# A column layer's tile loop: rows turned two tiles ahead, output product two tiles behind

## What is computed

```
cols     = gelu(einsum('bsd,cdn->bscn', x, W_cols) + b_cols)     # 16 columns of 64 neurons
cols     = cols * weights[..., None]                             # one column kept per token
y        = cols.reshape(B, S, -1) @ proj_w + proj_b + x
out      = (y - mean(y)) * rsqrt(var(y) + 1e-05) * ln_g + ln_b
```

## Time and profile before

| | us |
|---|---|
| median of 3 runs (lowest, highest) | 1276.15 (1275.35, 1277.19) |
| the profiled execution's own time | 1278.38 |
| its span, first to last instruction | 1276.6 |
| the tile loop on PE, first transposes to the end of the last output product | 1165.8 to 1260.5 |
| last DVE instruction | ends 1268.2 |
| last store issued by POOL | 1269.4 |

### The profile page before, as it was taken

One profiled execution on the slowest core, in us unless ns is written; L12 is line 12 of the kernel. 1 busy time (PEld: TensorE's weight loads), 2 busy tenths in 40 slices (PEclk: granted clock), 3 DMA queues, 4 the chain that ended last, 5 costly groups with the idle time before them and its releaser, 6 DMA issues. The chain is left out here.

```text
span 1276.6 us, 33231 instructions
## 1 busy us (share of the span) xinstructions
PE 1180.1 (92%) x12565; PEld 852.2 (67%) x12565; DVE 963.9 (76%) x1677; ACT 674.7 (53%) x1497; POOL 587.9 (46%) x835
## 2 busy tenths in 40 slices
PE   4798899999999999589999999999999996998994
PEld 4575688778778778356666666666676664754662
DVE  7778656765765775878888888888888885776776
ACT  5854122123113113267788778877877775332673
POOL 1426888888888000543333333333333320815674
PEclk9998899999999999779999999999999999889997
DMA  8605444545545110785656566656666620434661
GB/s 219 160 1 187 123 145 137 173 137 145 168 136 164 47 37 1 113 146 95 96 92 96 98 99 99 99 99 99 99 98 99 97 40 2 116 116 143 196 183 43
DMA packets 111754, 141.82 MB, mean 111 GB/s; under 512 B 10317, under 2 KB 94776, under 8 KB 109380
## 3 DMA queue, kind: packets, MB, share of 16 engines
q1 hardware_dynamic: 97796, 96.15, 37.2%
q0 software_dynamic: 13824, 43.84, 12.0%
HBM read 105.79 MB, written 30.49 MB: 107 GB/s over the span
## 5 line engine op out<-in xcount | busy, mean ns | idle before, releaser
L1269 DVE TENSOR_REDUCE s_neg_max<-banks 112x3 bf16<-112x1461 f32 (+1 forms) x192 | 290.2, 1512 | 44.8 <-PE banks L1385 44.7
L1183 ACT ACTIVATE s_prob<-banks 128x448 f32<-128x448 f32 x512 | 272.8, 545 | 91.1 <-PE banks L1411 76.3
L714 DVE TENSOR_TENSOR s_m<-banks,s_base 128x512 f32<-128x512 f32 x256 | 161.2, 683 | 100.6 <-PE banks L868 100.3
L1411 PE MATMUL banks<-s_q_t,s_k_t 112*128 112x112 bf16 x2048 | 186.5, 215 | 1.1 <-ACT s_prob L1183 1.0
L1411 PEld LDWEIGHTS banks<-s_q_t,s_k_t 112*128 112x128 bf16 x2048 | 124.1, 98 | 72.6 <-issue 50.6
L868 PE MATMUL banks<-s_gate_sel,s_tw 64*128 64x256 f32 x1024 | 132.5, 399 | 1.3 <-DVE s_m L714 1.3
L911 PE MATMUL banks<-s_m,s_act_t 128*112 128x256 f32 x512 | 128.2, 388 | 1.5
L1427 PE MATMUL banks<-s_prob,s_v 128*32 128x112 f32 (+1 forms) x4096 | 125.8, 263 | 0.7 <-ACT s_prob L1183 0.7
L893 PEld LDWEIGHTS banks<-s_x_t,s_m 128*128 128x128 f32 x1024 | 116.7, 192 | 10.6 <-issue 7.6
L893 PE MATMUL banks<-s_x_t,s_m 128*128 128x112 f32 x1024 | 122.4, 278 | 0.0
L808 ACT ACT_TABLE_LOAD x8 | 10.3, 1283 | 206.5 <-PE banks L893 206.5
(11 more groups left out here) (312 smaller groups left out, 2209.7 us busy)
## 6 DMA issues: line engine op xcount, KB each, us to landing
k_parts<-s_k_split POOLq DMA_DIRECT2D x64, 281.2 KB, 3.6
s_k_t<-k_parts SPq DMA_DIRECT2D x32, 562.5 KB, 8.0
s_tw<-in_tw SPq DMA_DIRECT2D x16, 1024.0 KB, 5.3
s_k_raw<-in_ctx_k POOLq DMA_DIRECT2D x64, 187.5 KB, 3.7
s_k_t<-k_parts SPq DMA_DIRECT2D x32, 375.0 KB, 5.3
s_v_raw<-in_ctx SPq DMA_DIRECT2D x32, 256.0 KB
s_src<-in_ctx SPq DMA_DIRECT2D x8, 896.0 KB, 15.6
s_k_t<-k_parts SPq DMA_DIRECT2D x32, 187.5 KB, 9.0
```

The source lines that it names most:

```text
L714: nc.vector.tensor_tensor(dst[:, :, :, rows_], got, base[:, :, rows_].unsqueeze(2).broadcast_to([P, 2, B, HR]), ALU.add).then_inc(S["merge ...
L1183: nc.scalar.activation(prob[t % 2][:, c, :], w.bank(SCORE + n % SRING, P, TILE), ACT.Exp, scale=DH ** -0.5).then_inc(S["exp_done"], 1)
L1269: nc.vector.tensor_reduce(neg_max[half][:, ROWS + first:ROWS + end, 0], w.banks[0:T, MAX:MAX + end - first, 0:NKEY], AX.X, ALU.max, negate ...
L1411: last = nc.tensor.matmul(w.bank(SCORE + n % SRING)[:, s * T:(s + 1) * T], k_t[k][0:ROWS_MAX, h, c * P:(c + 1) * P], q_t[k][0:ROWS_MAX, h, :],
```

## The change

Evacuated rows (`x_tt`) and gelu outputs (`hid_c`) get three buffers each, the weights six. Transposes go to bank 0, 1 or 7, two tiles ahead of the column product; the output product comes two tiles behind it. The dummy matmuls move from the end of a turn into `turn`, ahead of the transposes, and write the bank that the transposes then overwrite. `column` and its waits, `SQRT_LAG`, the order on DVE and POOL and the dummy matmuls outside the loop stay.

```diff
-    SEMS, RING_W, N_SUBS = 8, 4, 2 * SLOT_TILES
+    SEMS, RING_W, DEEP, N_SUBS = 8, 6, 3, 2 * SLOT_TILES
...
-        x_tt = [sb(f"s4_x_tt{k}", [P, KD, P]) for k in range(2)]
+        x_tt = [sb(f"s4_x_tt{k}", [P, KD, P]) for k in range(DEEP)]
-        hid_c = [sb(f"s4_hid_c{k}", [N4, 2, P]) for k in range(2)]
+        hid_c = [sb(f"s4_hid_c{k}", [N4, 2, P]) for k in range(DEEP)]
...
+        def turned_at(n):
+
+            return w.bank((0, 1, 7)[n % 3])
+
+        def column_at(n):
+
+            return w.bank(2 + n % 2, N4, P)
...
-                for k in range(2):
+                for k in range(DEEP):
                     nc.gpsimd.memset(hid_c[k][:], 0.0)
...
                 def evacuate_row(n):
                     wait(act, "turned", n + 1)
-                    wait(act, "col_ps", n - 1)
+                    wait(act, "col_ps", n - DEEP + 1)
                     for kk in range(KD):
-                        last = nc.scalar.activation(x_tt[n % 2][:, kk, :], w.bank(n % 2)[:, kk * P:(kk + 1) * P],
+                        last = nc.scalar.activation(x_tt[n % DEEP][:, kk, :], turned_at(n)[:, kk * P:(kk + 1) * P],
...
                     wait(act, "col_ps", n + 1)
-                    wait(act, "y_ps", n - 1)
+                    wait(act, "y_ps", n - DEEP + 1)
...
                 evacuate_row(0)
+                evacuate_row(1)
                 for n in range(N_TILES):
-                    if n + 1 < N_TILES:
-                        evacuate_row(n + 1)
+                    if n + 2 < N_TILES:
+                        evacuate_row(n + 2)
                     gelu(n)
                     if n >= SQRT_LAG and group_end(n - SQRT_LAG):
                         roots(n - SQRT_LAG)
...
                 def turn(n):
                     pe.wait_ge(row_in[n % SEMS], 16 * (n // SEMS + 1))
-                    wait(pe, "x_tt_done", n - 1)
+                    wait(pe, "x_tt_done", n - 2)
+                    busy(2, turned_at(n))
                     for kk in range(KD):
-                        last = nc.tensor.transpose(w.bank(n % 2)[:, kk * P:(kk + 1) * P], row(n)[:, kk * P:(kk + 1) * P],
+                        last = nc.tensor.transpose(turned_at(n)[:, kk * P:(kk + 1) * P], row(n)[:, kk * P:(kk + 1) * P],
...
                 turn(0)
+                turn(1)
                 for n in range(N_TILES):
-                    if n + 1 < N_TILES:
-                        turn(n + 1)
+                    if n + 2 < N_TILES:
+                        turn(n + 2)
                     column(n)
-                    if n >= 1:
-                        output(n - 1)
-                    busy(2)
+                    if n >= 2:
+                        output(n - 2)
+                output(N_TILES - 2)
                 output(N_TILES - 1)
```

More of the change, by code:

```diff
@@ L1734, in gelu @@
                     wait(act, "col_ps", n + 1)
-                    wait(act, "y_ps", n - 1)
+                    wait(act, "y_ps", n - DEEP + 1)
                     for k, c in enumerate(cs):
                         at = slice(k * SUB, (k + 1) * SUB)
-                        last = nc.scalar.activation(hid_c[n % 2][:, k, at], w.bank(2 + n % 2, N4)[:, at], ACT.Gelu,
+                        last = nc.scalar.activation(hid_c[n % DEEP][:, k, at], column_at(n)[:, at], ACT.Gelu,
                                                     bias=b_cols[:, bass.ds(c, 1)])
@@ L1992, in _, with busy @@
                     last.then_inc(S["logit_ps"], 1)
-                def busy(count, cols=512):
+                def busy(count, bank=w.bank(7)):
                     for _ in range(count):
-                        nc.tensor.matmul(w.bank(7, P, cols), ones16[:], keep[:].rearrange("t c b -> t (c b)")[:, 0:cols],
-                                         start=True, stop=True)
+                        nc.tensor.matmul(bank, ones16[:], keep[:].rearrange("t c b -> t (c b)"), start=True, stop=True)
                 wait(pe, "counting", 2)
@@ L2043, in column @@
                         for kk in range(KD):
-                            last = nc.tensor.matmul(w.bank(2 + n % 2, N4)[:, at], w_tile[n % RING_W][:, k, kk, :],
-                                                    x_tt[n % 2][:, kk, at], start=(kk == 0), stop=(kk == KD - 1))
+                            last = nc.tensor.matmul(column_at(n)[:, at], w_tile[n % RING_W][:, k, kk, :],
+                                                    x_tt[n % DEEP][:, kk, at], start=(kk == 0), stop=(kk == KD - 1))
                     last.then_inc(S["col_ps"], 1)
@@ L2054, in output @@
                     for k, c in enumerate(cs):
-                        last = nc.tensor.matmul(w.bank(4 + n % 3, P, D), hid_c[n % 2][:, k, :], proj[:, bass.ds(c * D, D)],
+                        last = nc.tensor.matmul(w.bank(4 + n % 3, P, D), hid_c[n % DEEP][:, k, :], proj[:, bass.ds(c * D, D)],
                                                 start=(k == 0), stop=(k == 1))
```

## The result

The changed kernel takes 1280.82 us (median of 7 runs, 1278.53 to 1284.41), the kernel before beside it 1276.48. The ratio is 1.0039, 95% interval 1.0023 to 1.0055: slower by 5.0 us (2.9 to 7.0). Forecast: +2.9 us, 1279.0, range 1273.4 to 1282.3.

A forecast was written before the change was run, and what follows sets the result against it. PE was taken to bound the tile loop, after following the weights before column 8, with DVE the bound at the end. The terms summed to -1.6 + 6b, +2.9 us with b = .75: 1279.0 us, range 1273.4 to 1282.3.

The forecast's parts named there:

- One group with its roots: Tile loop: ACT waits at the root for DVE's later radicands, holding register loads; gelu 18 ends late, output 18 stalls .75 us.
- b: PE's stall ahead of an output, once per four-tile group, six between columns 8 and 33: .75 us, against .53 before.
- The value from the rows of an ordinary group: Choice of .75 us for the stall per group, between bounds of .2 and 1.3.
- Rival (3): Held chains in the loop are longer through slow register loads: stall 1.0 to 1.3 us, +4.4 to +6.2; chance .19.
- The start: Before column 8 weights come when they came, PE runs 1.2 us behind them, and column 8 stays at 1188.0.
- The end: After column 33 DVE decides: tile 33 is summed 6.0 us after it, 4.4 before; the longer lag gives back 1.6.
- past the last column: The stall of the group after those ending at 7 to 27 would fall after column 33, so it wasn't counted.
- DVE's chain is the same: From the summing of tile 33 on, DVE takes the same 12.0 us as before, the stores behind it.
- No cost of dummies and buffers: Loop: moved dummies taken as 0 (up to .54 us a turn if they collided); third buffers and their clearing cost nothing.
- Rival (1): ACT's register loads run during the root's wait: stall .2 us, sum -.4, 1275.7, no slower; chance .20.
- Rival (2): Start: weights come early enough that PE doesn't trail by 1.2 us; the stall vanishes too: -2.8, 1273.4; chance .11.
- The sum: Whole kernel: -1.6 + 6b us, with b = .75 +2.9 us; 1281.3 for the profiled execution, 1279.0 for the median.

The follow-up runs named there:

- e8: Changed kernel with roots three turns after a group's end up to tile 27 and outputs caught up to one behind from column 32: .9972, 1272.9 us.
- e6: Changed kernel with PE's two register loads for the output issued ahead of the column product's waits: .9981 of the kernel before, 1274.1 us.
- e11: Changed kernel with four weight buffers instead of six: 1.0062 of the kernel before.
- e10: Changed kernel with ACT's two register loads for the next gelu ahead of the root's wait, run again for its profile; first measured at 1.0011, 1277.9 us.
- e12: Changed kernel with PE's register loads ahead of the column's waits and outputs caught up to one behind from column 32: .9997, 1276.1 us.
- e7: Changed kernel with roots three turns after up to tile 27, PE's loads ahead of the column's waits, outputs caught up from column 32: .9993, 1275.6 us.
- e3: Changed kernel with output products one tile behind again, rows still turned two ahead: 1.0008 of the kernel before.
- e1: Changed kernel with roots taken three turns after a group's end instead of two: .9990 of the kernel before, 1275.2 us.
- e5: Kernel before with output products two tiles behind and three gelu output buffers, nothing else: 1.0529, 1344.27 to 1346.73 us.
- e9: Kernel before with outputs two behind, three gelu output buffers and more dummies in the first four turns: 1.0065, 1282.78 to 1288.12 us.

## Why the prediction was right, and where its sizes were off

- **One group with its roots: right, shown.** The wait at the root was .56 in the group followed (forecast .59; .40 in the mean), released by DVE; the loads came after it; gelu 18 ended at 6.97 (6.8); output 18 waited .69 (.75). Each link taken away by itself removes the stalls: the wait in e8, PE's loads in e6.
- **The size of b: low by a quarter.** 66.44 = 60.6 + 6b gives b = .97, not .75, worth 1.3 us: the upper edge of the forecast's .5 to 1.0. The six gaps make 5.1 of these 5.8 us; the rest is small delays that the formula puts on b as well. Three groups stall .67 to .73, as forecast, and three .95 to 1.09. There the slow register loads decide that were put at the upper end: for output 22, where the wait is 1.09, the two loads of PE are

```profile
L2058 PEldq TENSOR_LOAD <-s_column_of x2: 321/366/411, 1230.0 to 1230.8; - x2
```

  and those of ACT ahead of it

```profile
L1741 ACTq TENSOR_LOAD <-s_column_of x2: 277/392/507, 1226.6 to 1227.3; - x2
```

  Ahead of outputs 14 and 30, the other two, a load of PE took 503 and 407 ns; in the three shorter stalls no load of the chain took over 350. In e11, whose loop is the same, five of the six stalls are .87 to 1.00, each with a load of 394 to 520 ns in its chain, and the one with none over 333 is .62. "The value from the rows of an ordinary group" was the term that was mis-sized: half of the groups or more aren't ordinary. Rival (3) named these loads, with .19; its 1.0 to 1.3 for b was not reached.
- **The start: off by .5, the good way.** Column 8 was put where it was; it came .54 earlier. That the change did this isn't shown: in the changed kernel, e10, e8 and e11, where SP issues its loads up to there alike, within .11 us, it comes 29.12 to 30.21 us after the first fetch (29.66 before). That PE trails the weights by its own loads was right: with these loads first it comes after 28.36 to 28.89 us (e12, e6, e7).
- **The end: right in kind.** Tile 33 summed 5.62 after column 33 (forecast 6.0). The roots of tile 31, now a turn later on DVE, hold the gelu of tile 34 in the same way as in every group, and output 34 waits 1.89 (.56 before). The prediction had this stall "past the last column" and gave it no price: +.63, the term left out when "DVE's chain is the same" was taken.
- **No cost of dummies and buffers: right** by e3. (A pair of dummies takes .44 us of PE in the trace of before, 1210.27 to the transposes at 1210.71, not the .54 of the prediction, which put the term at 0.) POOL's first store came at 1190.16, 2.0 later against the first fetch than before (forecast 2.4), and nothing waited for it.
- **Rival (1) falls.** The rule of the Trainium skill (Perfetto Trace Analysis, Per-instruction lifecycle, DVE / Act Engine Instruction) would let the loads run during the root's wait. The trace says otherwise, and it decides: they began at 1215.9, after the root at 1215.74, as in every group. Rival (2) had half of its first part, and not the second.
- **The sum.** The profiled execution came 1.8 us above its forecast of 1281.3: +1.3 from b, +.6 from output 34, -.5 from the start, -.4 at tile 33, and +.76 that arose ahead of the loop. These partly cancel. No run ties the last to the change: the first fetch comes at 1153.25 in e6 and at 1155.48 in e7.

## What to carry to other kernels

When a product is moved back by a turn, everything computed from it moves too: move the consumers' due times (here the roots' distance) with it, or they turn into waits. Count what an in-order queue holds behind each new wait, register loads above all: reading the two indices ahead of the wait was worth as much as removing it (.9981 in e6, .9990 in e1, within their intervals). After the stall is gone, look at the next queue's pace before adding up gains: here SP's loads, 2.48 us a tile, are just slower than PE's 2.42.

## What the hardware did that was not expected

- In e5 PE was busy 1.26 us of 4, and the granted clock went from 1.00 to .50 and stayed there, though the records show PE busy 65.00 us of 65 in the loop; the five runs were 5.3% slower. Fourteen more dummies in the idle turns (e9) kept it at 1.00. The same order of outputs cost some 67 us with the idle turns at the start, and 8.3 without them.
- Register loads took 296 to 350 ns in one group and up to 507 (ACT) and 503 (PE) in others; each of the longer stalls has such a load ahead of it. Why some are slow is open.
- On ACT, loads put ahead of a table load held it back by .95 us (e10), although the engine was idle.
